# Six of the 128 adjacency loads are issued as two transfers, of 120 rows and of 8 rows

## What is computed

```python
def reference(x, adj, L0_gnn_weight, L0_gnn_att_weight, L1_gnn_W_msg, L1_gnn_b_msg,
              L1_gnn_W_ih, L1_gnn_W_hh, L1_gnn_b_ih, L1_gnn_b_hh):
    h = jnp.maximum(_layernorm(x, axis=-1), 0.0)
    x = x + _L0_gnn_ref(h, adj, L0_gnn_weight, L0_gnn_att_weight)
    h = jnp.maximum(_layernorm(x, axis=-1), 0.0)
    x = x + _L1_gnn_ref(h, adj, L1_gnn_W_msg, L1_gnn_b_msg, L1_gnn_W_ih, L1_gnn_W_hh, L1_gnn_b_ih, L1_gnn_b_hh)
    return x
...
    # _L0_gnn_ref: four heads of 32 features
    wh = jnp.matmul(h_mat, weight).reshape(n, H, OUT_PER_HEAD)
    e = jax.nn.leaky_relu(logit_parent[:, None, :] + logit_child[None, :, :], ALPHA)
    att = jnp.where(adj[..., None] > 0, e, NEG_BIG)
    att = jax.nn.softmax(att, axis=1)
    h_prime = jnp.einsum('njh,jhf->nhf', att, wh)
...
    # _L1_gnn_ref
    agg = adj @ states
    msg = jax.nn.relu(agg @ W_msg.T + b_msg)
    return _gru_cell(msg, states, W_ih, W_hh, b_ih, b_hh)
```

## Time and profile before

| | us |
|---|---|
| median of 3 runs | 955.73 |
| lowest and highest run | 954.14, 957.25 |
| profiled execution, its own time | 955.24 |
| span of that execution, first to last instruction | 953.2 |
| piece 1 to the last piece: ACT starts on them at | 23.6 to 738.1 |

### The profile page before, as it was taken

One profiled execution on the slowest core, in us unless ns is written; L12 is line 12 of the kernel. 1 busy time (PEld: TensorE's weight loads), 2 busy tenths in 40 slices (PEclk: granted clock), 3 DMA queues, 4 the chain that ended last, 5 costly groups with the idle time before them and its releaser, 6 DMA issues.

```text
span 953.2 us, 12291 instructions
## 1 busy us (share of the span) xinstructions
PE 690.6 (72%) x3349; PEld 427.8 (45%) x3349; DVE 748.8 (79%) x3099; ACT 657.5 (69%) x669; POOL 525.6 (55%) x518
## 2 busy tenths in 40 slices
PE   1686765677776857676777777696868677999976
PEld 0353423445444434343454444354435474566643
DVE  8667686889878889797888888777878786898763
ACT  1786765979797878888787868787877644445522
POOL 4021166173545637373736475756677577777771
PEclk9997887988978798788787788868887579999998
DMA  9999999999999999999999999999996102333231
GB/s 293 418 418 420 420 412 405 406 409 416 412 419 408 410 399 399 407 400 408 396 408 380 405 395 404 407 400 392 388 402 238 29 5 72 72 82 83 53 77 51
DMA packets 55749, 305.49 MB, mean 320 GB/s; under 512 B 13825, under 2 KB 31442, under 8 KB 39296
## 3 DMA queue, kind: packets, MB, share of 16 engines
q1 hardware_dynamic: 27936, 274.74, 70.9%
q0 software_dynamic: 17152, 23.15, 8.5%
q10 hardware_dynamic: 10592, 6.82, 2.4%
HBM read 295.65 MB, written 12.71 MB: 323 GB/s over the span
## 4 chain that ended last, share of the span: by engine, by line
DMA 49%; ACT 16%; PE 10%; POOL 10%; DVE 7%; issue 5%; SPq 1%; ACTq 0%; POOLq 0%; DVEq 0%
DMA adj_in<-in_adj 49%; ACT ind L697 14%; POOL adj_in L606 8%; PE ps L968 3%; POOL adj_in L597 1%; PE ps L947 1%; POOL val L587 1%; DVE cand L1455 1%; SPq L507 1%; PE ps L1041 1%; DVE rows_in L1407 1%; PE ps L989 1%; PE ps L965 1%; ACT adj_in L747 0%; PE ps L1188 0%
## 5 line engine op out<-in xcount | busy, mean ns | idle before, releaser
L697 ACT ACTIVATE ind<-adj_in 128x4096 bf16<-128x4096 int32 x128 | 462.3, 3612 | 96.6 <-DMA adj_in<-in_adj 90.4
L968 PE MATMUL ps<-ind,bit_w 128*128 128x512 bf16 x1024 | 301.3, 439 | 65.3 <-ACT ind L697 65.1
L587 POOL DMA_INDIRECT val<-in_adj,val_idx x144 | 152.1, 1056 | 205.1 <-DVE val_idx L1669 152.1
L569 POOL DMA_INDIRECT rows_in<-wh_table,idx x180 | 193.0, 1072 | 61.8 <-issue 61.8
L968 PEld LDWEIGHTS ps<-ind,bit_w 128*128 128x128 bf16 x1024 | 110.5, 111 | 224.5 <-ACT ind L697 83.6
L1455 DVE MAX8 cand<-ps 128x8 f32<-128x256 f32 x256 | 90.9, 417 | 34.2 <-PE ps L968 33.8
L606 POOL DMA_INDIRECT adj_in<-g_table,idx x80 | 81.6, 1021 | 24.4 <-issue 24.1
L965 PE MATMUL ps<-idx_r,idx_w 128*128 128x512 bf16 x128 | 60.3, 471 | 21.4 <-ACT ind L697 21.3
L1021 PE MATMUL ps<-rows_in,ident 128*128 128x132 f32 x120 | 34.7, 385 | 47.7 <-DVE rows_in L1572 47.7
L613 POOL DMA_DIRECT2D wh_table<-rows_in x16 | 12.1, 757 | 85.8 <-DVE rows_in L1407 85.8
L1021 PEld LDWEIGHTS ps<-rows_in,ident 128*128 128x128 f32 x120 | 26.7, 274 | 54.9 <-DVE rows_in L1572 54.9
(11 more groups left out here) (313 smaller groups left out, 1550.4 us busy)
## 6 DMA issues: line engine op xcount, KB each, us to landing
adj_in<-in_adj SPq DMA_DIRECT2D x128, 2048.0 KB, 18.2
wh_table<-rows_in POOLq DMA_DIRECT2D x16, 264.0 KB, 8.5
out<-rows_in SPq DMA_DIRECT2D x16, 256.0 KB, 2.4
g_table<-g_buf ACTq DMA_DIRECT2D x15, 256.0 KB, 25.8
rows_in<-wh_table,idx POOLq DMA_INDIRECT x180, 6.6
val<-in_adj,val_idx POOLq DMA_INDIRECT x144
adj_in<-g_table,idx POOLq DMA_INDIRECT x100, 2.7
edges_more<-g_table,idx POOLq DMA_INDIRECT x28, 6.2
```

The costliest lines, as they stand in the source:

```text
L569: nc.gpsimd.indirect_dma_start(out=rows_in[:, s % 2, t, k, :], out_offset=None, in_=wh_table, in_offset=bass.IndirectOffsetOnAxis(ap=idx[: ...
L587: nc.gpsimd.indirect_dma_start(out=val2[:, s, k:k + 1], out_offset=None, in_=adj_values, in_offset=bass.IndirectOffsetOnAxis(ap=val_idx2[: ...
L697: nc.scalar.activation(ind[:, (tile * 2 + half) % IND, :], adj_in[:, slot, 0:b - a].bitcast(I32), ACT.Relu, bias=1.0, scale=-1.0, accum_ou ...
L968: ins = nc.tensor.matmul(o, bit_w[:, b, :], ind[:, (tile * 2 + half) % IND, c0:c0 + HALF], start=False, stop=(b == BITS - 1))
```

## The change

Pieces 14, 34, 54, 74, 94 and 114, counted from zero, are loaded by two transfers in place of one: rows 0 to 119 of the tile into partitions 0 to 119, and rows 120 to 127 into partitions 120 to 127. Both add 16 to the buffer's semaphore. So the count that ACT waits for is 16 higher from such a piece on, for the pieces in that buffer. Pieces 14, 34, ... all go through buffer 2 (14 % 4 = 2, as 20 is a multiple of 4). Nothing else is changed.

```diff
+WIDE = 120
+SPLIT = range(14, 2 * T, 20)
...
+        def piece_landed(n):
+            return 16 * (n // SLOTS + 1 + sum(m % SLOTS == n % SLOTS and m <= n for m in SPLIT))
...
                 def load(tile, half, slot):
                     a, b = CUT[half], CUT[half + 1]
-                    sp.dma_start(adj_in[:, slot, 0:b - a], adj[bass.ds(tile * P, P), a:b]).then_inc(adj_sem[slot], 16)
+                    if tile * 2 + half in SPLIT:
+                        sp.dma_start(adj_in[0:WIDE, slot, 0:b - a], adj[bass.ds(tile * P, WIDE), a:b]).then_inc(adj_sem[slot], 16)
+                        sp.dma_start(adj_in[WIDE:P, slot, 0:b - a], adj[bass.ds(tile * P + WIDE, P - WIDE), a:b]).then_inc(adj_sem[slot], 16)
+                    else:
+                        sp.dma_start(adj_in[:, slot, 0:b - a], adj[bass.ds(tile * P, P), a:b]).then_inc(adj_sem[slot], 16)
...
-                    act.wait_ge(adj_sem[slot], (s * 2 + (2 * t + half) // SLOTS + 1) * 16)
+                    act.wait_ge(adj_sem[slot], piece_landed(tile * 2 + half))
```

## The result

The changed kernel takes 1029.76 us as the median of 4 runs (1028.77 to 1033.44). The kernel before, run beside it, takes 956.49. The ratio is 1.076, with a 95% interval of 1.072 to 1.080: 73 us slower, where the forecast was 10 us faster. The profiled execution has a span of 1026.8 us against 953.2.

What follows compares the result with a forecast made beforehand. One late DMA engine was taken to bound the load stream. Sparing it 30.2 us let the other fifteen's 15.5 us idle time, less 3.8 for extra rows, give 11.7, cut to 10 by allowances: 955.73 to 945.7 us, range 939 to 960.

Steps and rivals of the forecast that it cites:

- What bounds the kernel: Adjacency load stream: one DMA engine ends some 10 us after the other fifteen; ACT waits 90.4 us in all for loads.
- The 15.5: Estimated idle time, in us, of each of the other fifteen DMA engines over the load stream, from the DMA shares.
- How the rows are shared: Split pieces: 120 rows go eight each to fifteen engines, 8 rows one each to eight engines.
- the price of the 120-row transfer: Split pieces: the 120-row load costs 5.04 us an engine like a whole load, so 0 extra.
- a slow transfer: Rival at the six split pieces: engines writing 120 rows hinder each other; 974 us at double time; chance 0.11.
- which engine is spared: Split pieces: the engine that gets none of the 120 rows was taken to be the late one, spared 5.04 us each.
- The 30.2 us of relief: Load stream: engine time taken off the late engine over six split pieces, so that it ends at 708 us.
- the gain of 11.7 us: End of the load stream: earlier by 11.7 us, bounded by eight engines with extra rows, done at 726.3 instead of 738.0.
- the 10 us of the sum: Load stream ends 10 us earlier, after allowing for idle time that stays; the rest of the kernel moves forward as a whole.
- the other case: Rival at split pieces: wrong engine spared; late engine gets one row more each, 3.8 us later in all, 959.5 us; chance 0.08.

Runs made afterwards that it cites:

- three-row copies: Kernel before with whole loads, plus three rows copied HBM to HBM, unused, behind every fourth piece (31 copies), on three engines: 958.4 us, ratio 1.001.
- eight-row copies: Kernel before with whole loads, plus 8 rows copied HBM to HBM, unused, behind every fourth piece (31 copies), on eight engines: 977.2 us, ratio 1.020.
- seven-row copies: Kernel before with whole loads, plus 7 rows copied HBM to HBM, unused, behind every fourth piece (31 copies), on seven engines: 981.4 us, ratio 1.025.

## Why the prediction was wrong

**What bounds the kernel** was read rightly. One engine is late, the other fifteen have idle time, and ACT waits for that one. The increments of the semaphores show it directly. The three-row copies put the idle time at 20 us or more. The 15.5 were too few, at least in part because the share from 726 to 738 counts POOL's gathers as work of the fifteen: it gives them 8.5 us of idle time there, and their increments come 9.5 to 12.0 us ahead.

**How the rows are shared** was right as to the numbers: 15 engines and 8, by the 42 packets and the 23 increments. I had assumed it; the trace of before had no such load.

**The step that failed first** is the price of the 120-row transfer, taken "like the nearest row, the whole load with 5.04 us an engine, so at 0 extra". It is 5 us more on every engine that takes part: 216 GB/s in place of 420, 1.24 us a row in place of 0.62. All loads in the trace of before had 128 rows, so the nearest row was no evidence for another row count. I had a slow transfer as a rival, with the other end of the range at 5.04 us a transfer and 974 us, and gave it 0.11. That other end, double time, was an assumption of mine with no row behind it. The runs show that writing to the buffer is what is slow. Among 16, 64, 112, 120 and 128 rows only 128 are free of it: of 420 GB/s, 120 and 64 rows get half (215 and 206), 112 rows six tenths and 16 rows a third. Why just these shares, no run shows.

**The second step that failed** is which engine is spared. It is not the late one, as the 0.34 share at the end of the changed kernel, the increments of its split pieces and the copies show. The 30.2 us of relief went to an engine that had idle time anyway, and the gain of 11.7 us was not there to be had. No run shows a relief of the late engine, on which the 10 us of the sum rest; that the spared engine would be the late one was my assumption. I had the other case as a rival of its own, at 959.5 us for a late engine that gets one row more, and gave it 0.08.

**Both rivals came true together, and the size was off again.** 5.04 us of slowness at six pieces make 30 us; measured were 73, 12.2 a piece. The relief is missing and so is not taken off. What is left over is the late engine. Its increments in the changed kernel show how. It raises the semaphore for pieces 51 to 53 at 327.1, 334.8 and 345.1 us, for its 120-row share of piece 54 at 355.3, and for the extra row at 356.2: 7.7, 10.3, 10.2 and 0.9 us, where the pieces around them, 50 and 51 and 55 to 57, take it 4.7 to 6.1. At pieces 72, 73 and 74 it is 10.0, 10.0 and 10.4. The others are done with piece 53 at about 330 us and with the 120 rows of piece 54 at about 340.

So when the late engine is 8 us or more behind, it is still writing its rows of the whole pieces 52 and 53 when the others are at the 120 rows of piece 54, and these rows are slow as well (7.7 and 10.3 us for the pieces). Then its own share of the 120 rows is slow too, 10.2 us, when the others are back at whole loads. These are two slow stretches, and the first can take more than one piece. ACT's two waits of 6.0 and 7.0 us, before piece 53 and before piece 54, are these. While the engine is 2 to 3 us behind, at pieces 14 and 34, the two overlap more: the landing of the split piece falls behind by 7.5 and 10 us, and ACT by 8. Why the late engine is slow while the others write their 120 rows, no run isolates; that it is slow twice, and that the cost goes with the place in the stream, is shown.

**Chances.** The two mechanisms were priced as alternatives, each alone. Nothing excluded both, and together they take away the gain and add the loss: at least 955.7 + 30 + 4 = 990 by my own numbers, outside the range.

**What stays open.** How the rows of such a transfer are dealt out to the engines, and why 120 and 64 rows get half the rate, 112 more and 16 less. Why the engine is late. The instruction queues have not been placed on an engine by any run. A kernel that spares the late engine wasn't tried: all ways of leaving it out that I know need transfers of other than 128 rows, whose cost at the buffer (11 us a piece) is many times what there is to gain.

## What to carry to other kernels

A large load into the on-chip buffer should, by these runs, have all 128 rows, or be cut by columns, which was free (a ratio of 1.000); transfers of 16 to 120 rows ran at a third to six tenths of 420 GB/s, at DMA shares of 0.92 to 1.07. So a full DMA share said nothing about the rate: look at GB/s beside it. And before work is taken off "the slow engine", find out which one it is, by giving small extra copies to some engines and not to others. Three engines with idle time took 31 rows each for nothing (a ratio of 1.001), the late one did not (1.025 with seven rows), and the copy's semaphore showed by a late last increment, 10.5 and 12.6 us after the others, that the slow one was among them.

## What the runs showed of the hardware

- Loads of 128 rows x 16 KB: 420 GB/s. Into the same buffer, 120 rows 213 and 216, 112 rows 259 and 267, 64 rows 206 on average, 16 rows 139 to 152 GB/s in the first 8 us, all at DMA shares of 0.92 to 1.07. A row of 16 KB takes 0.62 us in a whole load and 1.24 in one of 120 rows. 128 rows of 8 KB, 436 GB/s.
- 120 rows copied from HBM to HBM behind the loads: 382 to 429 GB/s around the first copy, 4.7 us a copy.
- A transfer of one row of 16 KB was cut into 16 packets, one an engine; three rows went to three engines.
- One engine of 16 fell behind the others. In the kernel before its rows landed 1.5 us after those of the other fifteen at piece 14, 6.9 us at piece 54 and 9.5 us at the last piece; in the other kernels the gap at the last piece was 6.6 to 11.4 us, and with the three-row copies 8.6 us after twelve and 1.1 us after fifteen. It was one of the eight that took a row in the eight-row copies and of the seven in the seven-row copies, and none of the three in the three-row copies. The three had some 20 us of idle time or more in 738, by an estimate from 31 rows of 0.62 us and the 1.1 us.
- While fifteen engines write 120 rows, the late one, still at whole pieces, is slow too: 7.7 to 10.3 us a piece at pieces 52, 53, 72 and 73 of the changed kernel, where in the kernel before a piece comes 4.7 to 7.1 us after the one ahead of it.
